# Another order for the 48 steps of a turn of the heads

## The chip, the cores and the metric

The kernel runs on one core of a Trainium2 chip. The metric is the device time of one execution in microseconds, taken as the median of several runs. A profiled execution shows where that time goes: TensorE (PE) does the matrix products, VectorE (DVE), ScalarE (ACT) and GpSimd (POOL) the rest, and SyncE (SP) issues nearly all DMAs. Each engine works through its own instructions in the order in which they are written, and they meet only at semaphores.

## The reference, cut to what matters

The layer is `x + attention(layernorm(x)) + experts(layernorm(x))` for x of 2 x 2048 x 512. The attention has 16 heads of width 128. Its queries, keys and values go through a causal convolution of four taps and a silu, and then a recurrence over the 2048 positions (a gated delta rule):

```
def step(S, inps):
    qt, kt, vt, at, bt = inps
    Sk = jnp.einsum('bhvk,bhk->bhv', S, kt)
    err = Sk - vt
    S = at[..., None, None] * S - bt[..., None, None] * (err[..., None] * kt[:, :, None, :])
    ot = jnp.einsum('bhvk,bhk->bhv', S, qt)
    return (S, ot)
```

The output `ot` is normalised over its 128 channels, multiplied by a sigmoid gate and projected by Wo. The experts are a mixture of 16, four for each of 512 tokens.

## The kernel before, in words

`prepare` normalises and turns x, computes the gates alpha and beta, and does the experts. `heads` does the attention, and `project` most of the product with Wo. The change is in the order of `heads` alone.

**Turns.** `heads` treats one head of one batch row at a time (32 heads in all), each in four groups (g = 0 to 3) of 512 positions. A turn is one such group, so there are 128, and a few turns around them that fill and drain the pipeline. In the loop three heads, twelve turns, are written out. The recurrence is computed in chunks of 128 positions, four in a group. Inside a chunk it becomes the inverse of a triangular 128 x 128 matrix and a few products, and from chunk to chunk the state S (128 x 128) is carried.

**Stages.** A turn works on several groups at once, each at another stage: `proj` is four groups ahead of the chain, `inv` three, `mid` two, `late` one, `chain` is the current group, and `ln` is one group behind. So what a turn computes is used in a later step of the same turn or in one of the next turns.

**Steps.** Each turn has 48 steps (`STEPS`), and every engine's `turn` function runs over all 48 and looks at each step which of its operations stand there. The constants in lines 54 to 79 say so: `L_AT = 22` puts the product L at TensorE's step 22. A step is a place in an engine's queue, and no time: two engines that are at the same step number are not at the same moment, unless a semaphore makes it so. Within one step the operations follow in the order of the code.

**TensorE** issues in each step one projection matmul of 512 columns (`project_some`, L1540): 48 for the four projections of a group, 12 each, three for each of four blocks of rows (high x high, high x low, low x high parts). Twelve projections fill a bank; its three banks are taken again when the convolution or the tanh has read them. Around these stand:
- the chain (`chain_step`, L1629 to L1659), 12 links, three for each of the four chunks c. Link 3c: the product of S and k (L1629), after which VectorE forms R (L1273). Link 3c+1: the product of R and TT (L1642), then q_gamma with S (L1647) into the output bank, after which ScalarE copies Wc (L1449). Link 3c+2: the product of Wc and k_rows (L1653) and of Wc and AT (L1659), after which VectorE updates S (L1286) and ScalarE copies the output `o` (L1456). `CHAIN` gives the step of each link.
- two visits of small products for the triangular inverse (`visit`): visit 0 (L1594, L1605, L1616) waits for the transpose `Tnb` (L1294), visit 1 (L1597, L1608, L1619) for what follows from visit 0 one turn earlier. Visit 0 is preceded by its waits and by that step's projection.
- A (`A_AT`, L1669), the turned keys (`KT_AT`, L1688) and values (`VT_AT`, L1694), L (`L_AT`, L1705), and the turned normalised output (`ON_TURN_AT`, L1716).

**The 16 x 16 block inverse** goes round through several engines. TensorE makes L, VectorE LT (L1351), ScalarE copies its diagonal blocks (`DIAG_AT`, L1400), GpSimd masks and adds them to Lc (`LC_AT`, L1170 and L1174), SP stores Lc into DRAM (`base_d`, L977, twice), waits for the stores, and loads it back spread over the partitions as Lb (L983). GpSimd solves with it in 15 pairs of small operations (`SOLVE_AT`, L1158 and L1165; a pair depends on the one before) and writes TTb (`T16P_AT`, L1180). VectorE transposes it to Tnb (`T16_AT`, L1294), which visit 0 needs. A late step of `SOLVE_AT` (over 24) works on the group loaded in that turn, an early one on the group of the turn before.

**GpSimd** also computes the power for the normalisation (`POW_AT`, `hrstd`, L1186), q_gamma (`QG_AT`, L1192), the gated output oG (`OG_AT`, L1200) and, in four places over two groups, the low parts of the next head's weights (`CUT_AT`, L1142; ScalarE's high parts, L1362, stand at the same steps). VectorE's normalised output `on` (`ON_AT`, L1318) waits for the power.

**ScalarE** further makes the first tap (`TAP_AT`, L1466 and L1468), kT, qT and vT, the sigmoid gate, diag_b (`DIAGB_AT`, L1393), the turned output oT (`OT_AT`, L1491), the value rows, and copies of the inverse's blocks (`PLACE_AT`, `TN_PLACE_AT`, `MT32_AT`, `TT64_AT`, `MT64_AT`, `TT128_AT`).

**SP** issues in each turn, in this order: gamma and scale when the chain has let them go, beta when diag_b is made, alpha when decay is made, the base blocks (two stores, a wait, one load), the next weights in one of four turns, and the store of oG.

GpSimd's operations stand in this form in its `turn`:

```
for s in range(STEPS):
    if s in SOLVE_AT and (proj if s > STEPS // 2 else inv):
...
    if proj and s == LC_AT:
...
    if inv and s == T16P_AT:
...
    if ln and s == POW_AT:
```

Of the kernel before, what the change touches and what calls it, by code (L numbers as in the profile page):

```python
# [50 lines left out]
LEAD = 0  # L51
PE_SLOT = 0

CHAIN = {2: 0, 5: 1, 10: 2, 12: 3, 16: 4, 22: 5, 24: 6, 27: 7, 31: 8, 37: 9, 42: 10, 47: 11}
PJ_OF = [[0, 1, 2, 0], [1, 2, 0, 1], [2, 0, 1, 2], [0, 1, 2, 1]]
PJ_FREED = [[(1, 0), (1, 3), (1, 2), (0, 0)], [(1, 1), (1, 2), (1, 3), (0, 0)],
            [(1, 1), (1, 2), (1, 3), (0, 0)], [(1, 1), (1, 2), (1, 3), (0, 1)]]
A_AT, KT_AT, VT_AT, ON_TURN_AT, L_AT = 12, 4, 14, 30, 22
VISIT_AT = {28: 0, 2: 1}
SOLVE_AT = {44: (0, 1), 45: (1, 4), 0: (4, 5), 3: (5, 6), 4: (6, 11), 5: (11, 13), 6: (13, 15)}  # L60
T16P_AT, POW_AT, QG_AT, OG_AT, DIAG_AT, LC_AT = 11, 13, 26, 40, 24, 22
AT_AT, K_AT, T16_AT, TN64_AT, DECAY_AT, LT_AT = 16, 7, 24, 9, 18, 22
BN_AT, AGGR_AT, ON_AT = 4, 11, 25
YB_AT, TT_AT = 38, 0
CONV_AT = {11: (0, 0), 12: (0, 1), 14: (0, 2), 26: (1, 0), 27: (1, 1), 30: (1, 2), 38: (2, 0), 42: (2, 1), 44: (2, 2)}
VSILU_AT, GATE_AT, DIAGB_AT, VROWS_AT, KSILU_AT, QSILU_AT, OT_AT = 3, 12, 7, 15, 18, 38, 31
PLACE_AT = {30: (0, 1), 14: (2, 3)}
TN_PLACE_AT = 1
MT32_AT, TT64_AT, MT64_AT, TT128_AT = 46, 5, 36, 3
O_AT = {7: 0, 22: 1, 38: 2, 2: 3}  # L70
TAP_AT = {7: 0, 25: 1, 38: 2}
TILES, TILE0 = 6, 4
TILE_CUT_AT = {25: (0, 1), 33: (1, 1), 42: (2, 1), 5: (3, 0)}
TILE_AT = 3
CUT_AT = {(3, 28): 0, (3, 34): 1, (3, 41): 2, (0, 22): 3}
ROUND_E, ROUND_T, RING = 4, 11, 3
EXPERT_AT = {0: 2, 3: 3, 6: 4, 8: 5}
WO_AT, W_AT = {1: 0, 3: 1, 5: 2, 7: 3}, 9
# [656 lines left out]
def heads(nc, bank, ident, pow_half, xT_hi_d, xT_lo_d, gates_d, base_d, oT_d, x_hi, x_lo, w_raw, w_cut, weights, taps, ln_w, ln_b,  # L735
# [10 lines left out]
    with ExitStack() as ctx:  # L746
# [466 lines left out]
        def _(dve):  # L1213
# [13 lines left out]
            def turn(dve, hh, g, n, chain, late, mid, inv, proj, ln, tile=None):  # L1227
                at = counter(hh, g)
                par, cur = (g + 1) % 2, g % 2
                for s in range(STEPS):  # L1230
# [27 lines left out]
                    if late and s == K_AT:  # L1258
# [4 lines left out]
                                          decay[:, (n + 1) % 3, 0:m, C:C + 1].to_broadcast([P, m, D]), ALU.mult).then_inc(k_done, 1)  # L1263
                    if chain and s in CHAIN:
                        k = CHAIN[s]
                        c, r = k // 3, k % 3
# [92 lines left out]
        def _(act):  # L1359
# [6 lines left out]
            def turn(act, hh, g, n, chain, late, mid, inv, proj, ln, tile=None):  # L1366
# [4 lines left out]
                for s in range(STEPS):  # L1371
# [66 lines left out]
                    if chain and s == TT128_AT:  # L1438

                        act.wait_ge(late_done, at(2, 1))  # L1440
                        for odd in range(2):
                            rows = slice(64, 128) if odd else slice(0, 64)
                            act.activation(TT[0:64, n % 3, odd::2, 64:128], w64[rows], ACT.Copy, scale=-1.0)\
                               .then_inc(tt128_done, 1)
                    if chain and s in CHAIN and CHAIN[s] % 3 == 1:
                        k = CHAIN[s]
                        act.wait_ge(chain_done, at(12, 0, k + 1))
# [62 lines left out]
        def _(pe):  # L1510
            def turn(pe, hh, g, n, chain, late, mid, inv, proj, ln, tile=None):
# [151 lines left out]
                for s in range(STEPS):  # L1663
# [14 lines left out]
                    if s in VISIT_AT:  # L1678
                        visit(VISIT_AT[s])
                    if chain and s in CHAIN:  # L1680
                        chain_step(CHAIN[s])
                    if late and s == KT_AT:
# [202 lines left out]
```

## Time and profile before

| | |
|---|---|
| median of 3 runs | 3532.4 us (3527.67 to 3541.74) |
| the profiled execution's own time | 3523.38 us |
| its span | 3521.8 us |
| mean granted TensorE clock | 0.995 |
| busy: PE, DVE, ACT, POOL | 98%, 68%, 67%, 55% of the span |
| `prepare`, before the first projection of the heads | 417.5 us |
| `heads`, its 128 turns and the drain | 417.5 to 3228 us |
| `project` | from 3228 us |

An instruction's record has its start and its length. The matmuls are pipelined, and a record of one covers more than its place in the queue: 512 columns are recorded with 0.39 to 0.48 us and follow one another every 0.23 us. So the distances between starts are read, and not the lengths. "Idle before" is time in which the engine had nothing running ahead of an instruction, and the name behind it is what ended the wait.

### The profile page before, as it was taken

To read this page: it belongs to the slowest core of one execution; us is meant where nothing else is said; L and a number is where in the kernel's file an instruction comes from. 1 tells how busy PE (TensorE), PEld (TensorE's weight loads), DVE (VectorE), ACT (ScalarE), POOL (GpSimd) and SP (SyncE) were. 2 spreads that over 40 slices of the span, in tenths; PEclk is the share of its full clock that TensorE was granted. 3 is DMA by queue.
4 is the path that set the end of the run, shared out by engine and by line. 5 is a ranking of instruction groups with operands and counts; after the bars stand their busy time and mean duration, and the time that the engine had idled before them with its cause. 6 is when DMAs were issued, how large, how long until landed. Compare 5 with 4: busy or idle time off the path is not lost. (4 is left out here: it accounts for less than half of the span.)

```text
span 3521.8 us, 105822 instructions
## 1 busy us (share of the span) xinstructions
PE 3444.3 (98%) x32308; PEld 2888.2 (82%) x32308; DVE 2401.3 (68%) x5785; ACT 2352.4 (67%) x6448; POOL 1927.6 (55%) x4905
## 2 busy tenths in 40 slices
PE   8999989999999999999999999999999999999998
PEld 7788768888888888888888888888888888877887
DVE  6656557777777777777777777777777777753222
ACT  4443467777777777777777777777777777762111
POOL 3323256666666666666666666666666666653000
PEclk9999999999999999999999999999999999999999
DMA  8654433333333333333533333333333333444543
GB/s 309 222 194 152 168 84 80 78 86 86 83 77 80 78 83 83 77 77 80 149 101 84 82 78 77 80 78 81 85 79 77 80 81 86 115 151 135 146 145 101
DMA packets 427683, 375.91 MB, mean 107 GB/s; under 512 B 191984, under 2 KB 323056, under 8 KB 421248
## 3 DMA queue, kind: packets, MB, share of 16 engines
q1 hardware_dynamic: 424000, 362.46, 37.8%
q8 instruction: 261, 4.28, 0.5%
q0 software_dynamic: 2080, 6.82, 0.5%
q14 instruction: 286, 2.34, 0.2%
q10 hardware_dynamic: 1056, 0.02, 0.0%
HBM read 292.62 MB, written 76.58 MB: 105 GB/s over the span
## 5 line engine op out<-in xcount | busy, mean ns | idle before, releaser
L1332 DVE SCALAR_TENSOR_TENSOR conv<-bank,tap,conv 128x512 f32<-128x512 f32 x1152 | 863.5, 750 | 183.8 <-ACT conv L1468 159.5
L1158 POOL TENSOR_TENSOR prods<-Lb,Tc 128x60 f32<-128x60 f32 (+14 forms) x1920 | 482.8, 251 | 557.3 <-DMA Lb<-base_d 413.5
L1540 PE MATMUL bank<-hx_hi,w_lo 128*128 128x512 f32 x1536 | 663.5, 432 | 0.0
L1540 PE MATMUL bank<-hx_lo,w_hi 128*128 128x512 f32 x1536 | 644.3, 419 | 14.4 <-DVE Tnb L1294 14.4
L1540 PE MATMUL bank<-hx_hi,w_hi 128*128 128x512 f32 x1536 | 645.5, 420 | 0.0
L1165 POOL TENSOR_TENSOR Tc<-Tc,prods 128x56 f32<-128x56 f32 (+13 forms) x1792 | 462.2, 258 | 141.1 <-POOL prods L1158 1.6
L1540 PEld LDWEIGHTS bank<-hx_lo,w_hi 128*128 128x128 f32 x1536 | 292.5, 190 | 45.6 <-DVE Tnb L1294 16.5
L1540 PEld LDWEIGHTS bank<-hx_hi,w_lo 128*128 128x128 f32 x1536 | 292.5, 190 | 31.9
L1540 PEld LDWEIGHTS bank<-hx_hi,w_hi 128*128 128x128 f32 x1536 | 293.0, 191 | 30.7 <-DVE conv L1332 6.1
L1400 ACT ACTIVATE same<-LT 32x128 f32<-32x128 f32 x512 | 157.4, 307 | 180.8 <-DVE LT L1351 171.5
L1468 ACT ACTIVATE conv<-bank,tap 128x512 f32<-128x512 f32 x384 | 264.0, 687 | 12.5
L1273 DVE SCALAR_TENSOR_TENSOR R<-bank,scale_c,v_rows 128x128 f32<-128x128 f32 x480 | 166.5, 347 | 145.3 <-PE bank L1629 145.2
L1286 DVE SCALAR_TENSOR_TENSOR S<-S,gamma,bank 128x128 f32<-128x128 f32 x480 | 162.5, 339 | 144.3 <-PE bank L1653 143.2
L1456 ACT ACTIVATE o<-bank 128x128 f32<-128x128 f32 x512 | 142.0, 277 | 142.8 <-PE bank L1659 134.6
L1142 POOL TENSOR_TENSOR w_lo<-w_raw,w_hi 128x512 fp32r<-128x512 f32 x152 | 195.2, 1285 | 75.9 <-ACT w_hi L1362 74.4
L1540 PE MATMUL bank<-x_hi,w_lo 128*128 128x512 f32 x512 | 223.7, 437 | 1.5 <-issue 0.3
L1540 PE MATMUL bank<-x_hi,w_hi 128*128 128x512 f32 x512 | 215.9, 422 | 2.9 <-issue 1.4
L1540 PE MATMUL bank<-x_lo,w_hi 128*128 128x512 f32 x512 | 215.2, 420 | 1.5 <-DVE Tnb L1294 1.5
L1653 PEld LDWEIGHTS bank<-Wc,k_rows 128*128 128x128 f32 x960 | 181.5, 189 | 37.5 <-ACT Wc L1449 1.9
L1642 PEld LDWEIGHTS bank<-R,TT 128*128 128x128 f32 x960 | 170.8, 188 | 50.4 <-DVE R L1273 23.7
L1629 PEld LDWEIGHTS bank<-S,kT 128*128 128x128 f32 x960 | 169.9, 189 | 39.7 <-DVE S L1286 9.9
L1200 POOL TENSOR_TENSOR oG<-oT,gT 128x512 f32<-128x512 f32 x128 | 165.3, 1291 | 62.7 <-ACT oT L1491 62.7
(211 smaller groups left out, 8880.3 us busy)
## 6 DMA issues: line engine op xcount, KB each, us to landing
Lb<-base_d SPq DMA_DIRECT2D x128, 512.0 KB, 4.7
gamma<-gamma_d SPq DMA_DIRECT2D x128, 258.0 KB, 3.6
alpha<-alpha_d SPq DMA_DIRECT2D x128, 256.0 KB, 3.2
oT_d<-oG SPq DMA_DIRECT2D x128, 256.0 KB, 4.2
gu_raw<-in_gate_up SPq DMA_DIRECT2D x16, 1408.0 KB, 6.4
o_raw<-oT_d SPq DMA_DIRECT2D x13, 1024.0 KB, 6.9
w_raw<-oT_d SPq DMA_DIRECT2D x12, 1024.0 KB, 7.2
dn_raw<-in_down SPq DMA_DIRECT2D x44, 256.0 KB, 6.9
```

Source lines behind the costliest of these rows:

```text
L1142: pool.tensor_tensor(w_lo[:, i], w_raw[:, i], w_hi[:, i].bitcast(F32), ALU.subtract).then_inc(wlo_done, 1)
L1158: pool.tensor_tensor(prods[:, :, i + 1:], Lb[:, i, :, i + 1:], Tc[:, :, i:i + 1].to_broadcast([P, G, SB - 1 - i]), ALU.mult)\
L1165: pool.tensor_tensor(Tc[:, :, i + 1:], (sel if i == 0 else Tc)[:, :, i + 1:], prods[:, :, i + 1:], ALU.subtract).then_inc(solve_done, 1)
L1200: pool.tensor_tensor(oG[:], oT[:], gT[:, (n - 1) % 6], ALU.mult).then_inc(oG_done, 1)
L1273: dve.scalar_tensor_tensor(out=R[:], in0=CO[:, 0:D], scalar=scale[:, cur, c:c + 1], in1=v_rows[:, cur, c], op0=ALU.mult, op1=ALU.add)\
L1286: dve.scalar_tensor_tensor(out=S[:], in0=S[:], scalar=gamma[:, cur, c, C:C + 1], in1=CO[:, 2 * D:3 * D], op0=ALU.mult, op1=ALU.add)\
L1332: dve.scalar_tensor_tensor(out=conv[i][:, to], in0=PJ[PJ_OF[g][i]][:], scalar=tap[:, i, j + 1:j + 2], in1=conv[i][:, to], op0=ALU.mult, op ...
L1468: act.activation(conv[i][:, KS - 1:], PJ[PJ_OF[g][i]][:], ACT.Copy, scale=tap[:, i, 0:1])\
L1540: last = pe.matmul(dst, a[:, i, k], b[:, k], start=(j == 0), stop=(j == 3 * KC - 1))
L1629: pe.matmul(CO[:, 0:D], kT[:, n % 6, chunk(c)], S[:], start=True, stop=True).then_inc(chain_done, 1)
L1642: pe.matmul(CO[:, D:2 * D], TT[:, n % 3, c], R[:], start=True, stop=True)\
L1653: pe.matmul(CO[:, 2 * D:3 * D], k_rows[:, cur, c], Wc[:], start=True, stop=True)\
```

## The change

Only constants change: the step of each operation in a turn, for all engines. The operations, their operands, their number and the semaphores that they wait for stay. The stages and the loops stay too.

```diff
-CHAIN = {2: 0, 5: 1, 10: 2, 12: 3, 16: 4, 22: 5, 24: 6, 27: 7, 31: 8, 37: 9, 42: 10, 47: 11}
+CHAIN = {3: 0, 7: 1, 11: 2, 14: 3, 16: 4, 18: 5, 21: 6, 25: 7, 34: 8, 37: 9, 41: 10, 47: 11}
...
-A_AT, KT_AT, VT_AT, ON_TURN_AT, L_AT = 12, 4, 14, 30, 22
-VISIT_AT = {28: 0, 2: 1}
-SOLVE_AT = {44: (0, 1), 45: (1, 4), 0: (4, 5), 3: (5, 6), 4: (6, 11), 5: (11, 13), 6: (13, 15)}
-T16P_AT, POW_AT, QG_AT, OG_AT, DIAG_AT, LC_AT = 11, 13, 26, 40, 24, 22
-AT_AT, K_AT, T16_AT, TN64_AT, DECAY_AT, LT_AT = 16, 7, 24, 9, 18, 22
-BN_AT, AGGR_AT, ON_AT = 4, 11, 25
-YB_AT, TT_AT = 38, 0
-CONV_AT = {11: (0, 0), 12: (0, 1), 14: (0, 2), 26: (1, 0), 27: (1, 1), 30: (1, 2), 38: (2, 0), 42: (2, 1), 44: (2, 2)}
-VSILU_AT, GATE_AT, DIAGB_AT, VROWS_AT, KSILU_AT, QSILU_AT, OT_AT = 3, 12, 7, 15, 18, 38, 31
-PLACE_AT = {30: (0, 1), 14: (2, 3)}
-TN_PLACE_AT = 1
-MT32_AT, TT64_AT, MT64_AT, TT128_AT = 46, 5, 36, 3
-O_AT = {7: 0, 22: 1, 38: 2, 2: 3}
-TAP_AT = {7: 0, 25: 1, 38: 2}
+A_AT, KT_AT, VT_AT, ON_TURN_AT, L_AT = 16, 1, 15, 34, 23
+VISIT_AT = {35: 0, 3: 1}
+SOLVE_AT = {38: (0, 1), 39: (1, 2), 40: (2, 7), 41: (7, 10), 42: (10, 12), 44: (12, 13), 5: (13, 14), 14: (14, 15)}
+T16P_AT, POW_AT, QG_AT, OG_AT, DIAG_AT, LC_AT = 15, 11, 23, 34, 23, 16
+AT_AT, K_AT, T16_AT, TN64_AT, DECAY_AT, LT_AT = 16, 0, 29, 7, 19, 27
+BN_AT, AGGR_AT, ON_AT = 0, 3, 28
+YB_AT, TT_AT = 43, 1
+CONV_AT = {12: (0, 0), 14: (0, 1), 16: (0, 2), 31: (1, 0), 32: (1, 1), 34: (1, 2), 37: (2, 0), 38: (2, 1), 43: (2, 2)}
+VSILU_AT, GATE_AT, DIAGB_AT, VROWS_AT, KSILU_AT, QSILU_AT, OT_AT = 1, 28, 14, 16, 17, 41, 28
+PLACE_AT = {26: (0, 1), 18: (2, 3)}
+TN_PLACE_AT = 0
+MT32_AT, TT64_AT, MT64_AT, TT128_AT = 39, 5, 47, 1
+O_AT = {15: 0, 22: 1, 36: 2, 0: 3}
+TAP_AT = {10: 0, 22: 1, 33: 2}
...
-CUT_AT = {(3, 28): 0, (3, 34): 1, (3, 41): 2, (0, 22): 3}
+CUT_AT = {(3, 19): 0, (3, 29): 1, (3, 34): 2, (0, 19): 3}
```

## Rows read from the trace of the kernel before

**Rows 1.** Busy time by stretch, steady part: us, PE, PEld, DVE, ACT, POOL, PEclk, DMA
```profile
600.00:3010.00 2410.00, 2388.99 (x25787) 2024.19 (x25786) 1832.94 (x4785) 1880.62 (x5468) 1555.78 (x4216) 1.00 0.34 84
```

**Rows 2.** Waits of PE, 600 to 3010 us: total us, times, longest us
```profile
PE bank L1716 <- DVE on L1318: 13.5, 13, 1.7
PE bank L1540 <- DVE Tnb L1294: 4.4, 7, 0.9
```

**Rows 3.** Line 1170, 600 to 3010 us: ns min/median/max, first and last start
```profile
L1170 POOL TENSOR_TENSOR same<-same,same_c x114: 452/455/612, 615.0 to 3004.5; 128x128 f32<-128x128 f32 x114
```

**Rows 4.** Timeline of PE, visit 0 of two turns twelve apart: start, us
```profile
2522.23 0.42 PE L1594 MATMUL bank<-Tnb,LT 32*32 32x32 f32 x28
...
2773.52 0.42 PE L1594 MATMUL bank<-Tnb,LT 32*32 32x32 f32 x28
```

**Rows 5.** Timelines of POOL, DVE, PE and SP in a good turn
```profile
1649.09 0.24 POOL L1158 TENSOR_TENSOR prods<-Lb,Tc 128x4 f32<-128x4 f32 x1
...
1649.87 0.46 POOL L1180 TENSOR_TENSOR TTb<-Tc,same_c 128x128 f32<-128x128 f32 x1 [0.23 <-POOL Tc L1165]
...
1651.35 1.11 DVE L1318 TENSOR_SCALAR on<-o,hmv,hrstd 128x128 f32<-128x128 f32 x4
...
1652.01 0.42 PE L1594 MATMUL bank<-Tnb,LT 32*32 32x32 f32 x28
...
1653.51 0.60 PE L1716 MATMUL bank<-ident,on 128*128 128x128 f32 x4
...
1653.20 1.29 SPq L977 DMA_DIRECT2D base_d<-Lc  x2
1655.79 0.56 SPq L983 DMA_DIRECT2D Lb<-base_d  x1
```

**Rows 6.** Timelines of SP, POOL, DVE and PE around a bad turn
```profile
1737.94 1.23 SPq L977 DMA_DIRECT2D base_d<-Lc  x2
1741.87 0.56 SPq L983 DMA_DIRECT2D Lb<-base_d  x1
...
1757.45 1.02 POOL L1186 TENSOR_TENSOR hrstd<-hveps,pow_half 128x4 f32<-128x4 f32 x1
...
1759.25 1.19 POOL L1192 TENSOR_TENSOR q_gamma<-qT,gamma 128x512 f32<-128x512 f32 x1
...
1758.51 3.24 DVE L1318 TENSOR_SCALAR on<-o,hmv,hrstd 128x128 f32<-128x128 f32 x4 [0.67 <-POOL hrstd L1186]
...
1761.99 1.09 PE L1716 MATMUL bank<-ident,on 128*128 128x128 f32 x4 [1.75 <-DVE on L1318]
```

**Rows 7.** Busy time by stretch, just after that wait; the clock is third from last
```profile
1762.00:1766.00 4.00, 4.00 (x15) 3.58 (x16) 2.26 (x4) 2.32 (x6) 1.51 (x2) 0.60 0.52 135
```

**Rows 8.** Timelines of PE, DVE and ACT in the good turn, links of the chain
```profile
1650.95 0.40 PE L1540 MATMUL bank<-hx_hi,w_hi 128*128 128x512 f32 x1
1651.19 0.40 PE L1642 MATMUL bank<-R,TT 128*128 128x128 f32 x2
...
1650.71 0.34 DVE L1273 SCALAR_TENSOR_TENSOR R<-bank,scale_c,v_rows 128x128 f32<-128x128 f32 x1
...
1646.64 0.38 PE L1642 MATMUL bank<-R,TT 128*128 128x128 f32 x2
...
1647.06 0.28 ACT L1449 ACTIVATE Wc<-bank 128x128 f32<-128x128 f32 x1
```

**Rows 9.** Timelines of ACT in the good and the bad turn
```profile
1654.15 0.78 ACT L1491 ACTIVATE oT<-bank,lnb,lnw 128x512 f32<-128x512 f32 x1 [0.40 <-PE bank L1716]
...
1758.12 0.69 ACT L1468 ACTIVATE conv<-bank,tap 128x512 f32<-128x512 f32 x1
...
1758.86 0.63 ACT L1362 ACTIVATE w_hi<-w_raw 128x512 fp32r<-128x512 f32 x1
```

**Rows 10.** Waits of PE, 417 to 600 us
```profile
PE bank L1540 <- DVE Tnb L1294: 11.4, 3, 7.4
```

**Rows 11.** Waits of PE, 3010 to 3230 us
```profile
PE bank L1716 <- DVE on L1318: 4.0, 4, 1.4
```

## The prediction

> **What bounds the kernel now.** I read the busy time by stretch first, then TensorE's waits in each stretch, then the period of a turn, then an undisturbed turn and a late one side by side. In the steady part of the heads TensorE is busy 2389.0 of 2410.0 us with its clock at 1.00 [rows 1]: it is the bound, and its work is the same in both orders. An order can only win what TensorE does not work, or works at the lower clock. The waits name it: 13.5 us in 13 waits for `on` (the normalised output, L1318) before the four transposes of L1716, and 4.4 us in 7 waits for `Tnb` (L1294) before the small solving matmuls [rows 2]. L1170 runs once a turn: 113 turns from 615.0 to 3004.5 us are 21.15 us each [rows 3]. Twelve turns without such a wait, from 2522.23 to 2773.52 us, are 20.94 us each [rows 4]. So 0.21 us a turn, 113 x 0.21 = 24 us in all, is lost in a few bad turns; 20.94 us is the floor.
>
> What a bad turn is: in a good one [rows 5] GpSimd ends the block inverse with pair 14 (from 1649.09) and the write of TTb (1649.87 to 1650.33), then runs the power (`hrstd`, L1186; 1.02 us) to 1651.3, and VectorE starts `on` at 1651.35. `on` ends at 1652.46 and TensorE takes it at 1653.51: room 1.05 us. The matmuls of visit 0 start at 1652.01, 1.68 us after TTb is written. In a bad turn [rows 6] the load of the base blocks was issued 3.93 us after their stores (1737.94 to 1741.87), where the good one needs 2.59 (1653.20 to 1655.79): 1.34 us late. The thirty solving operations follow the load one by one, and in the next turn the power, which starts at 1757.45, is late by as much. Then comes a second loss: `on` takes 3.24 us for 1.12, since `q_gamma` starts on GpSimd at 1759.25 and runs beside it. TensorE waits 1.75 us, and its granted clock falls to 0.60 in the next four microseconds (1.2 GHz for a part of them) [rows 7].
>
> That row bears on a rule of the Trainium skill, SBUF — State Buffer, section "SBUF: two separate sides": VectorE in a two-port mode and GpSimd take one port pair in turn, each for a whole instruction. The trace agrees, by those 3.24 us.
>
> **The change, part by part.** Nothing is added or removed; only places of steps in each engine's queue move, and with them the waits.
>
> 1. *The solve.* GpSimd's pairs stood at 44, 45, 0, 3 to 6 and all before the power (13). Now pairs 0 to 12 stand at 38 to 44, pair 13 at 5, the power at 11, pair 14 at 14, TTb at 15, then Lc, q_gamma (23), oG (34). The load starts the pairs, as before. The product before it (L on TensorE) is at 23 instead of 22, a mean step of 20.94/48 = 0.44 us later, so masking, store, load and solve move by the same 0.44. But the power no longer stands behind pair 14 and TTb (1649.09 to 1650.33, 1.24 us). In the times of the good turn it ends at 1651.31 + 0.44 - 1.24 = 1650.5, and TTb is ready at 1650.33 + 0.44 + 1.02 = 1651.8.
> 2. *The users.* `on` is at 28 and `Tnb` behind it at 29 (before: Tnb 24, on 25), both after LT (27), which now ends at 1650.71 + 0.44 = 1651.15 (R followed it at 1650.71 [rows 8]). So VectorE has `on` from 1651.2 to 1652.3. The transposes move from 30 to 34: four projections more (0.23 each, the slot from 1650.95 to 1651.19), one step of the chain more (about 0.5) and visit 0 less (1653.51 - 1652.01 less two projections, 1.04), so 1653.51 + 0.92 + 0.5 - 1.04 = 1653.9. Visit 0 (35) follows at 1654.6. The room for a late power grows from 1.1 us to 1653.9 - 1650.5 - 1.1 = 2.3; that for a late TTb, less 0.3 for the transpose, from 1.4 to 1654.6 - 1651.8 - 0.3 = 2.5. A load late by 1.34 us fits into both.
> 3. *The collision.* q_gamma followed the late power by 0.8 us (1758.47 to 1759.25 [rows 6]). Now pair 14 and TTb stand between too, 1.24 us more, and `on` is over. Left are collisions with operations of 0.2 and 0.46 us, at most 0.9.
>
> Worth: 24 us of bad turns, less 2 left in some ten late ones (0 to 5): **-22 us**.
>
> 4. *Weight cuts.* GpSimd's cuts in the last group move from 28, 34, 41 to 19, 29, 34, the fourth from 22 to 19. The last no longer stands between the load and its solve; the ScalarE parts move alike. But ScalarE now has, between the transposes (34) and the copy `o` of chunk 2 (36): 0.64 from the transposes' start (1653.51 to 1654.15), oT 0.78, a cut 0.63, the tap 0.90 with its 0.20 us copy, a cut 0.63, the copy 0.28 and its release 0.1 [rows 9], 4.0 us end to end and 3.5 as they overlap; TensorE overwrites that bank at 41, 3.6 us after the transposes (seven projections, visit 0, three chain pairs). 0 to 0.4 us in 32 of 128 turns: 0 to 13 us. I take **+2**, near 3.5, since overlap is what the row shows (a tap of 0.69 and a Wc of 0.28 take 0.74, 1758.12 to 1758.86).
> 5. *The chain.* Its closest pairs were three steps apart and are now 16 to 18, with only two projections between. Needed: 0.42 (1646.64 to 1647.06) for the matmul, 0.28 for Wc, and 0.14 of release (R ends at 1651.05, L1642 starts at 1651.19), 0.84 us; there are 0.90 to 0.95 (0.82 from L1642 to visit 0 with one projection, and 0.23 more, less the 0.1 to 0.15 of entering the visit) [rows 8]. It fits if ScalarE is free: by then it has the tap, diag_b and a copy behind it since projection 11, 2.5 us of work in 4. I take 0 (0 to 0.1 in 128 turns, 0 to 13 us). The k_rows product (7 to 0) and the transposes before it (4 to 1) stand ahead of the chain's first R on VectorE; BN, k_rows, TTb, Tnb and R are 2.6 us and done about 0.3 us before TensorE asks at 7: 0.
> 6. *DMA queue.* SP's issues keep their order (gamma, scale, beta, alpha, base, oG). Beta waits for diag_b (7 to 14), alpha for decay (18 to 19), the oG store for oG (40 to 34). Each is used a turn or more later; hidden by that turn. If late, the base store behind alpha is the first to suffer.
> 7. *Start and end.* While the pipeline fills, Tnb costs 11.4 us in three waits [rows 10]. Visit 0 seven steps later puts 7 x 0.23 = 1.6 us of projections into the first; the others come a whole loop after it, with the same work between. **-1.6** (0 to -5). In the tail four waits for `on` cost 4.0 us [rows 11]; **-1** (-4 to +1).
>
> Sum: -22 + 2 - 1.6 - 1 = -22.6, about -22 us, against the profiled execution's own 3523.4. The median of the runs shown is 9 us above that; from 3532.4 the same sum gives **3510 us**.
>
> **The rivals.**
> - *Late stays late.* The load depends on Lc, Lc on GpSimd's last solve. From the load's issue to the end of the power it is 16.6 us (1741.87 to 1758.47 [rows 6]), from store to load 2.59 [rows 5], and the masking and Lc take 0.8: 20.0 us of a 20.9 us turn, in both orders. If lateness sums up over turns, less than half of the 22 is won: 3532 - 10 = 3522. For it: only 0.9 us a turn is recovered. Against: a bad turn is followed by good ones in the trace.
> - *The rule of the ports, for this order.* `on` now runs beside pair 14 and TTb in every turn. With 0.9 us of collision it ends at 1653.2, still ahead of 1653.9. In a turn with a load 1.34 us late it ends at 1650.5 + 1.34 + 1.1 + 0.9 = 1653.85, at the edge; some 0.4 us of wait in each of ten such turns: 3514. (The rule is the one cited above; it speaks against putting `on` there.)
> - *Small waits.* Parts 4 and 5 at half their bounds, +13 for my +2: 3521.
> - *Slower.* Place: ScalarE at the chain's step 16, behind diag_b (moved from 7 to 14) and the copy of chunk 0 (7 to 15). If it comes there later than TensorE, Wc waits and nothing lies between 16 and 18 to cover it: every microsecond is TensorE's. It decides from about 1.5 us of ScalarE lateness; with 0.35 us more, 128 x 0.35 = 45 us, less 22: 3555. For it: ScalarE works 1880.6 of 2410.0 us [rows 1] and the cuts fill it further in the last group. Against: at step 16 it is not.
>
> **How the numbers follow.** Forecast 0.45, late stays late 0.17, ports 0.10, small waits 0.15, slower 0.13. Low end: all 24, 5 and 4 us won from 3532, and 9 more if unprofiled runs have more bad turns: 3490. High end: nothing won and both small waits: 3536; only the slower rival and a little more lie outside. 0.5% is 17.7 us, about what a measurement of this kernel can tell: faster below 3514.7. Forecast nearly all, half of the ports and a little of the rest: 0.52. Slower 0.12, the rest 0.36.
>
> **What would show it.** Right: the waits of TensorE for `on` and `Tnb` in the steady part fall from 17.9 to under 4 us, no `on` over 2.5 us beside q_gamma, no clock loss there, 12 turns still 251.3 us. Wrong: TensorE idle before L1653 (ScalarE's Wc) or before L1659/L1647 (the copy `o`) by more than 5 us in all, a floor above 21.0, or the same 13 waits under another name.

## The result, and the profile after

The changed kernel takes **3482.2 us** (median of 6 runs, 3477.24 to 3483.19), the kernel before 3537.1 us beside it (6 runs, 3527.67 to 3548.68). The ratio is 0.9842, with a 95% interval of 0.9825 to 0.9858. The change was right in its sign, and the time lies under the low end of the predicted range, 3490 us. The profiled execution of the changed kernel took 3482.47 us with a span of 3480.9 us, its median; that of the kernel before 3523.38 us, 13.7 us under its new median. So the profiles account for 41 of the 55 us. The other 14 are in no trace: the runs before spread over 21 us and the changed ones over 6, which would fit a number of bad turns that varies from one execution to the next, but that is argued and not shown.

TensorE's busy time in the steady part of the changed kernel, in the columns of [rows 1]:

```profile
600.00:3010.00 2410.00, 2408.86 (x26220) 2065.55 (x26219) 1821.38 (x4865) 1907.86 (x5556) 1577.90 (x4291) 1.00 0.36 85
```

It is idle for 1.1 us where [rows 1] leave 21.0. The list of its waits in this stretch is empty: against [rows 2], neither `on` nor `Tnb` is there. L1170, once a turn (ns min/median/max, first and last start), against [rows 3]:

```profile
L1170 POOL TENSOR_TENSOR same<-same,same_c x116: 447/461/466, 613.3 to 3007.0; 128x128 f32<-128x128 f32 x116
```

115 turns in 2393.7 us are 20.81 us each, for 21.15. Visit 0 of two turns twelve apart, against [rows 4]:

```profile
1115.14 0.42 PE L1594 MATMUL bank<-Tnb,LT 32*32 32x32 f32 x28
...
1364.69 0.42 PE L1594 MATMUL bank<-Tnb,LT 32*32 32x32 f32 x28
```

That is 249.55 us, 20.80 a turn, where undisturbed turns took 20.94. This is what the prediction had ruled out.

A good turn of the changed kernel (timelines of GpSimd, VectorE, TensorE and SP), against [rows 5]:

```profile
901.76 1.01 POOL L1186 TENSOR_TENSOR hrstd<-hveps,pow_half 128x4 f32<-128x4 f32 x1
...
903.46 0.56 POOL L1180 TENSOR_TENSOR TTb<-Tc,same_c 128x128 f32<-128x128 f32 x1 [0.22 <-POOL Tc L1165]
...
903.35 1.26 DVE L1318 TENSOR_SCALAR on<-o,hmv,hrstd 128x128 f32<-128x128 f32 x4
...
905.87 0.60 PE L1716 MATMUL bank<-ident,on 128*128 128x128 f32 x4
...
905.74 1.27 SPq L977 DMA_DIRECT2D base_d<-Lc  x2
...
908.32 0.58 SPq L983 DMA_DIRECT2D Lb<-base_d  x1
```

The power ends 3.1 us ahead of the transposes (902.77 to 905.87); less 1.26 for `on`, which also had LT to wait for, 1.84 us are free, and before it was 1.05. The same rows two turns later, where the load is issued 4.30 us after its stores (2.58 is normal), against [rows 6]:

```profile
947.12 1.26 SPq L977 DMA_DIRECT2D base_d<-Lc  x2
...
951.42 0.57 SPq L983 DMA_DIRECT2D Lb<-base_d  x1
...
965.84 1.02 POOL L1186 TENSOR_TENSOR hrstd<-hveps,pow_half 128x4 f32<-128x4 f32 x1
...
967.55 0.50 POOL L1180 TENSOR_TENSOR TTb<-Tc,same_c 128x128 f32<-128x128 f32 x1 [0.23 <-POOL Tc L1165]
...
968.83 1.18 POOL L1192 TENSOR_TENSOR q_gamma<-qT,gamma 128x512 f32<-128x512 f32 x1
...
966.89 1.26 DVE L1318 TENSOR_SCALAR on<-o,hmv,hrstd 128x128 f32<-128x128 f32 x4 [1.24 <-POOL hrstd L1186]
...
968.39 0.63 PE L1716 MATMUL bank<-ident,on 128*128 128x128 f32 x4
```

The load is 1.72 us late, more than in [rows 6], and the power starts late enough for VectorE to wait 1.24 us. But `on` ends at 968.15, before q_gamma starts, and takes 1.26 us, not 3.24. TensorE comes for it at 968.39, and the whole turn takes 21.29 us, less than half a microsecond over its usual 20.82. The granted clock stays at 1.00.

Late loads have not become rarer. Of the turns 8 to 123 twelve follow a load that was issued over 3.2 us after its stores (2.59 is the median), and none of these twelve is longer than 21.3 us. In the kernel before there are seven such turns, and they take 22.7 to 25.0 us.

While the heads fill, TensorE waits 11.1 us in three waits for Tnb, for the 11.4 of [rows 10]. In the tail the four waits for `on` [rows 11], 4.0 us, are one of 0.5.

### The profile page after: what moved, and what is told of

The parts are those of the page before. It is cut to its first block and busy times, and to the rows that moved or that the text cites. A ratio compares the mean times of both kernels' runs of the same rounds, so it can differ in the third digit from the quotient of the medians.

```text
span 3480.9 us, 105791 instructions
## 1 busy us (share of the span) xinstructions
PE 3426.1 (98%) x32308; PEld 2900.5 (83%) x32308; DVE 2353.1 (68%) x5785; ACT 2348.0 (67%) x6448; POOL 1921.0 (55%) x4905
## 5 line engine op out<-in xcount | busy, mean ns | idle before, releaser
L1332 DVE SCALAR_TENSOR_TENSOR conv<-bank,tap,conv 128x512 f32<-128x512 f32 x1152 | 854.6, 742 | 57.0 <-ACT conv L1468 47.0
L1540 PE MATMUL bank<-hx_hi,w_lo 128*128 128x512 f32 x1536 | 652.1, 425 | 11.1 <-DVE Tnb L1294 11.1
L1540 PE MATMUL bank<-hx_hi,w_hi 128*128 128x512 f32 x1536 | 655.7, 427 | 0.8 <-DVE conv L1332 0.8
L1540 PE MATMUL bank<-hx_lo,w_hi 128*128 128x512 f32 x1536 | 637.1, 415 | 0.0
L1540 PEld LDWEIGHTS bank<-hx_hi,w_lo 128*128 128x128 f32 x1536 | 292.3, 190 | 43.2 <-DVE Tnb L1294 12.4
L1540 PEld LDWEIGHTS bank<-hx_hi,w_hi 128*128 128x128 f32 x1536 | 293.1, 191 | 29.3 <-DVE conv L1332 0.9
L1540 PEld LDWEIGHTS bank<-hx_lo,w_hi 128*128 128x128 f32 x1536 | 292.4, 190 | 29.9
L1449 ACT ACTIVATE Wc<-bank 128x128 f32<-128x128 f32 x512 | 142.0, 277 | 208.1 <-PE bank L1642 199.9
L1540 PE MATMUL bank<-x_hi,w_hi 128*128 128x512 f32 x512 | 218.4, 427 | 2.0 <-PEq L151 1.0
L1540 PE MATMUL bank<-x_hi,w_lo 128*128 128x512 f32 x512 | 217.6, 425 | 0.0
L1540 PE MATMUL bank<-x_lo,w_hi 128*128 128x512 f32 x512 | 213.0, 416 | 0.0
L1642 PEld LDWEIGHTS bank<-R,TT 128*128 128x128 f32 x960 | 180.7, 189 | 36.5 <-DVE R L1273 0.4
L1659 PE MATMUL bank<-Wc,AT 128*128 128x128 f32 x1024 | 197.8, 275 | 0.0
```

The lines of the kernel that those rows point to most:

```text
L1332: dve.scalar_tensor_tensor(out=conv[i][:, to], in0=PJ[PJ_OF[g][i]][:], scalar=tap[:, i, j + 1:j + 2], in1=conv[i][:, to], op0=ALU.mult, op ...
L1540: last = pe.matmul(dst, a[:, i, k], b[:, k], start=(j == 0), stop=(j == 3 * KC - 1))
L1642: pe.matmul(CO[:, D:2 * D], TT[:, n % 3, c], R[:], start=True, stop=True)\
L1659: pe.matmul(OB[:], AT[:, cur, c], Wc[:], start=first, stop=True).then_inc(out_done, 1)
```

## The experiments

The table has, beside each median, the ratio to the kernel before on the same chip, and three readings of the trace that the runs need. A turn is 48 projections, so every 48th start of L1540 opens one; the four figures are the median length of a turn in us by its place among the four of a head (first, second, third, last), over turns 8 to 123, and the sum is those 116 turns.

| kernel | us | ratio | first, second, third, last | sum |
|---|---|---|---|---|
| before | 3537.1 | 1 | 21.00, 20.99, 20.87, 21.20 | 2453.4 |
| changed | 3482.2 | 0.9842 | 20.63, 20.92, 20.82, 20.70 | 2414.5 |
| changed, other chip | 3478.3 | 0.9859 | 20.60, 20.91, 20.78, 20.69 | 2412.1 |
| before + `on` used later | 3538.4 | 1.0049 | 21.39, 21.04, 20.92, 21.32 | 2467.1 |
| before + power ahead of pair 14 | 3539.8 | 1.0057 | 21.18, 21.02, 21.23, 20.80 | 2464.0 |
| before + q_gamma later | 3613.8 | 1.0278 | 22.39, 21.01, 20.87, 22.88 | 2535.8 |
| before + visit 0 and Tnb later | 3641.5 | 1.0342 | 22.18, 22.09, 21.98, 21.90 | 2556.1 |
| before + visit 0 later | 3600.2 | 1.0198 | 21.20, 21.35, 21.23, 21.12 | 2528.2 |
| before + new cuts | 3565.7 | 1.0124 | 21.23, 21.00, 20.86, 22.51 | 2490.3 |
| before + delayed load | 3568.1 | 1.0127 | 21.00, 21.01, 22.67, 20.79 | 2491.5 |
| changed + delayed load | 3494.4 | 0.9912 | 20.60, 20.92, 20.92, 20.70 | 2426.0 |
| changed, power back | 3541.2 | 1.0053 | 20.92, 20.91, 20.78, 21.13 | 2460.5 |
| changed, cuts back | 3493.7 | 0.9911 | 21.12, 20.92, 20.82, 20.70 | 2429.9 |
| changed, third cut back | 3486.5 | 0.9901 | 20.93, 20.91, 20.78, 20.69 | 2421.1 |
| changed, fourth cut back | 3477.7 | 0.9876 | 20.61, 20.91, 20.78, 20.69 | 2413.4 |
| changed, chain back | 4172.7 | 1.1826 | 23.87, 27.22, 26.91, 27.41 | 3056.3 |
| changed, link 3 later | 3480.0 | 0.9859 | 20.65, 20.91, 20.79, 20.68 | 2413.8 |

The kernel before took 3522 to 3526 us (medians) on the chips of the experiments. The half width of a ratio's interval is 0.0016 to 0.0029, but 0.0050 with q_gamma later.

### One part of the change, put into the old order

**`on` used later.**

```diff
-ON_TURN_AT 30, OT_AT 31
+ON_TURN_AT 34, OT_AT 35
```

> The kernel before, with only TensorE's transposes of the normalised output moved from step 30 to 34 and ScalarE's copy of them from 31 to 35. If the room behind the power is what counts, the 13.5 us of waits for `on` in the steady part mostly go (the 4.4 us for Tnb stay), and the time falls by 15 to 22 us (ratio 0.994 to 0.996). If lateness only moves to the next turn, or q_gamma's collision is what costs, it falls by under 8 us.

TensorE's waits, 600 to 3010 us:

```profile
PE bank L1659 <- ACT Wc L1449: 2.8, 17, 0.2
...
PE bank L1716 <- DVE on L1318: 1.0, 3, 0.5
```

The waits for `on` are gone, and the kernel is 0.5% slower. The expected gain of 15 us or more is missed. The turns with cuts are longer (first 21.39, last 21.32). Of the 0.39 us that the first turn is longer, 0.32 are lost by its step 2, by the starts of L1540, so they come over from the last turn of the head before, where the transposes and the turned output behind them now stand beside ScalarE's weight cuts and a Wc. That ScalarE is the cause is argued from these places; no run here separates it.

**The power ahead of pair 14.**

```diff
-SOLVE_AT ... 6: (13, 15);  T16P_AT 11
+SOLVE_AT ... 6: (13, 14), 14: (14, 15);  T16P_AT 15
```

> The kernel before, with only GpSimd's order changed: the power stands before pair 14 and TTb (steps 13, 14, 15), as in the new order; nothing moves on the other engines. Room theory: waits for `on` fall, but TTb is 1.0 us later with visit 0 still at step 28, so waits for Tnb grow in every late turn; sum between -10 and +15 us. If it were the power's place alone that brought the gain, the ratio would be near 0.99.

```profile
PE bank L1540 <- DVE Tnb L1294: 16.0, 25, 2.1
...
PE bank L1716 <- DVE on L1318: 0.4, 1, 0.4
```

In the listed waits it is a trade: 13.5 us for `on` [rows 2] became 16.0 us for Tnb. In time the kernel is 17.6 us above the one before, a little over the expected 15. Whichever of the two GpSimd does second is late, as long as visit 0 stays at 28.

**q_gamma later.** This is no part of the change, which moves q_gamma the other way (26 to 23). It takes the collision away by itself.

```diff
-QG_AT 26
+QG_AT 41
```

> The kernel before, with only q_gamma moved behind oG on GpSimd (26 to 41), so that it can't run beside a late `on`. Collision theory: no `on` over 2 us remains, waits for `on` fall from 13.5 to about 5 us and the clock loss goes, ratio 0.993 to 0.996. Room theory alone: under 5 us either way. It can also lose, where q_gamma now delays the solve in turns with weight cuts.

```profile
PE bank L1659 <- ACT Wc L1449: 45.0, 27, 1.7
```

```profile
1719.74 0.72 ACT L1484 ACTIVATE qT<-conv,tap 128x512 f32<-128x512 f32 x1 [2.12 <-POOL q_gamma L1192]
```

With q_gamma away no `on` is over 587 ns and no wait for `on` is listed. But ScalarE writes the next qT at step 38 and may do so only when q_gamma has read the old one; in the turns with cuts it stood 2.12 us for it (the second row, a timeline of ScalarE), with Wc behind it in its queue, and TensorE behind Wc. The kernel loses 2.8%. That the waits for `on` go with the collision is shown; what the collision costs in time is not, since the new wait hides it.

**Visit 0 later, first try.**

```diff
-VISIT_AT {28: 0, ...};  T16_AT 24;  YB_AT 38;  MT64_AT 36
+VISIT_AT {35: 0, ...};  T16_AT 29;  YB_AT 43;  MT64_AT 47
```

> The kernel before, with only visit 0 moved from step 28 to 35 and what hangs on it (Tnb 24 to 29, behind `on`; Yb 38 to 43; MT64 36 to 47). Room theory: the waits for Tnb (4.4 us and the short ones of 0.15 us in g = 0) go, while those for `on` stay or fall a little because TensorE comes 1 us earlier to the transposes: they grow. Time between -10 and +30 us. If the floor of 20.94 us a turn falls to 20.8 here, visit 0's place is what set it; if it stays, it is the chain's spacing.

TensorE's waits, and VectorE in one turn:

```profile
PE bank L1540 <- DVE Tnb L1294: 56.7, 106, 0.7
```

```profile
1717.09 1.11 DVE L1318 TENSOR_SCALAR on<-o,hmv,hrstd 128x128 f32<-128x128 f32 x4 [0.28 <-POOL hrstd L1186]
...
1718.88 1.54 DVE L1332 SCALAR_TENSOR_TENSOR conv<-bank,tap,conv 128x512 f32<-128x512 f32 x2 [0.67 <-ACT conv L1468]
1720.33 0.30 DVE L1294 STREAM_TRANSPOSE Tnb<-TTb 128x128 f32<-128x128 f32 x1
```

Tnb moved behind two convolution steps on VectorE (26 and 27), which stand at 31 and 32 in the changed kernel. The edit tested that and not visit 0, and this theory was neither confirmed nor refuted by it.

**Visit 0 later, with Tnb at its place.**

```diff
-VISIT_AT {28: 0, ...};  YB_AT 38;  MT64_AT 36
+VISIT_AT {35: 0, ...};  YB_AT 43;  MT64_AT 47
```

> The old order with visit 0 alone moved from step 28 to 35 (with the copies that follow it, yB to 43 and MT64 to 47); Tnb stays at 24 on VectorE, ahead of on, which the earlier try of this had moved behind two convolutions. Theory: the bad turns are of the wait for on, which VectorE does after Tnb, so they stay: waits for on of 10 us or more, those for Tnb under 1 us, and 3517 to 3525 us. Rival: visit 0's old place was the reason, since it stands ahead of the transposes in the queue and costs room there: the transposes now come 1 us earlier in time and the waits for on grow to 20 us or more, 3530 us or more. Third: the floor of a turn falls to 20.80 us by visit 0's place: 3505 to 3512 us.

```profile
PE bank L1716 <- DVE on L1318: 48.6, 37, 4.3
```

The rival held. Visit 0 had given `on` some of its room: without it ahead, TensorE is at the transposes 1 us earlier, and a late power costs that much more. A second loss was expected by none: the second and third turns are 0.36 us longer without any listed wait. By the starts of L1540, 0.38 of it is lost between steps 30 and 32, where the transposes (30) and link 8 (31) stand. Links 7 (27) and 8 had visit 0 between them as cover; in the changed kernel they stand at 25 and 34. That the missing cover is the reason is argued from these places.

**The weight cuts at their new places.**

```diff
-CUT_AT = {(3, 28): 0, (3, 34): 1, (3, 41): 2, (0, 22): 3}
+CUT_AT = {(3, 19): 0, (3, 29): 1, (3, 34): 2, (0, 19): 3}
```

> The old order with only the weight cuts at their new places (19, 29, 34 in the last group, 19 in the first). In the run with the cuts back at their old places only the first turn of each head was longer, 21.12 for 20.60 us. Theory: ScalarE's cut at step 41 makes it late until the chain's link 1 in the next turn, in both orders. Then the first turn's median falls here from 21.00 to 20.5 to 20.7 us, the others stay at 20.99, 20.87 and 20.8 to 21.2, and the time is 9 to 14 us under the kernel before. Rival 1: the cuts' new places pay only in the new order, since here ScalarE at 29 and 34 has oT (31) and the diagonal copies too: the first turn's median falls by less than 0.1 us or the last one's rises by 0.3, and the time is 0 to 15 us above. Rival 2: GpSimd's third cut, no longer between the load and its solve, also takes bad turns away: 20 us or more under.

TensorE's waits; then GpSimd, VectorE and TensorE in a last turn of a head; then the stretch behind (PE, PEld, DVE, ACT, POOL, clock, DMA):

```profile
PE bank L1716 <- DVE on L1318: 34.6, 29, 1.7
```

```profile
1775.94 1.02 POOL L1186 TENSOR_TENSOR hrstd<-hveps,pow_half 128x4 f32<-128x4 f32 x1
1776.93 1.27 POOL L1142 TENSOR_TENSOR w_lo<-w_raw,w_hi 128x512 fp32r<-128x512 f32 x1
...
1776.99 3.24 DVE L1318 TENSOR_SCALAR on<-o,hmv,hrstd 128x128 f32<-128x128 f32 x4 [0.67 <-POOL hrstd L1186]
...
1780.48 1.09 PE L1716 MATMUL bank<-ident,on 128*128 128x128 f32 x4 [1.75 <-DVE on L1318]
```

```profile
1780.00:1784.00 4.00, 3.52 (x13) 3.22 (x14) 2.75 (x5) 0.78 (x1) 1.39 (x2) 0.57 0.36 97
```

The theory and Rival 2 have the sign wrong, and Rival 1 has the sign but not the size, 42 us for 0 to 15. GpSimd's cut at 19 starts right behind the power in all 29 last turns, and in 27 of them `on` starts with it: the collision of [rows 6], now without any late load. `on` takes the same 3.24 us: of its four pieces, 0.34 us each when undisturbed, one takes 1.29 beside the cut and one 1.21 beside q_gamma. TensorE waits the same 1.75 us, and its granted clock is 0.57 in the four microseconds behind. The last turn is 1.3 us longer. In the changed kernel pair 14 and TTb stand between the power and that cut.

### The late load, made on purpose

A small store of Lc into a DRAM buffer of its own, and a wait for its landing, between the stores and the load of the base blocks, in one of four turns. It moves the load by 1.5 us, 32 times. (Lines are shifted by 5: L1323 is L1318.)

```diff
+if g == 1:
+    sp.dma_start(extra_d, Lc).then_inc(extra_stored, 16)
+    sp.wait_ge(extra_stored, ...)
```

> The kernel before, with the load of the base blocks made late by one more small store and its landing (about 1.9 us) in one group of four (g = 1, 32 times), which adds no work to any other engine. Room theory: each of these costs what a bad turn costs, 1.5 to 4 us (q_gamma's collision and the clock included): 50 to 120 us over the kernel before.

> The changed kernel with the same late load in one group of four. Room theory: 2.3 us of room takes 1.9 us; under 0.7 us each, 0 to 20 us over the changed kernel, so a ratio to the kernel before still near 0.985 to 0.99. Rival (the floor alone brought the gain, and late loads cost the same in both orders): 50 us and more over the changed kernel.

Waits of TensorE, the old order and then the new:

```profile
PE bank L1721 <- DVE on L1323: 24.1, 30, 1.5
PE bank L1545 <- DVE Tnb L1299: 18.1, 30, 1.3
```

```profile
PE bank L1721 <- DVE on L1323: 3.9, 5, 1.7
```

The turn behind the delay (the third) grows from 20.87 to 22.67 us in the old order and from 20.78 to 20.92 in the new. Over the 116 turns that is 38 us against 12 to 14: with 29 delays in them 1.3 us each against 0.4 to 0.5. The first expectation is missed by a little (45 us over the kernel before, for 50 to 120); the second held (16 us over the changed kernel), and its rival is refuted.

### One part of the change, taken back

**The power behind pair 14 and TTb again.**

```diff
-SOLVE_AT ... 14: (14, 15);  T16P_AT 15, POW_AT 11
+SOLVE_AT ... 9: (14, 15);  T16P_AT 10, POW_AT 11
```

> The changed kernel with GpSimd's power put back behind pair 14 and TTb (steps 9, 10, 11), all else as changed. The power then ends 1.24 us later, at about the moment when `on` starts. Room theory: 1.1 us of room is still there behind it, so good turns cost nothing, and the few turns with loads late by 1.3 us or more lose 0.3 to 2 us each: 0 to 15 us over the changed kernel. If the power's place was the key, 25 us and more.

Waits of TensorE; the durations of `on` (ns min/median/max); GpSimd, VectorE and TensorE in one bad turn:

```profile
PE bank L1716 <- DVE on L1318: 18.6, 10, 3.0
```

```profile
L1318 DVE TENSOR_SCALAR on<-o,hmv,hrstd x452: 334/343/1304, 614.4 to 2991.0; 128x128 f32<-128x128 f32 x151
```

```profile
1664.54 1.02 POOL L1186 TENSOR_TENSOR hrstd<-hveps,pow_half 128x4 f32<-128x4 f32 x1
...
1666.35 1.26 POOL L1142 TENSOR_TENSOR w_lo<-w_raw,w_hi 128x512 fp32r<-128x512 f32 x1
1667.57 1.17 POOL L1192 TENSOR_TENSOR q_gamma<-qT,gamma 128x512 f32<-128x512 f32 x1
...
1665.60 3.23 DVE L1318 TENSOR_SCALAR on<-o,hmv,hrstd 128x128 f32<-128x128 f32 x4 [2.12 <-POOL hrstd L1186]
...
1669.07 0.63 PE L1716 MATMUL bank<-ident,on 128*128 128x128 f32 x4 [2.99 <-DVE on L1318]
```

This one edit gives all of the gain back, and the time is 0.5% above the kernel before. The power is late by pair 14 and TTb, and what follows it on GpSimd is no longer pair 14 and TTb but the mask, a cut and q_gamma, beside which `on` takes 3.23 us. But the ten listed waits are not all of it. The median first and last turns of a head are 0.32 and 0.44 us longer than in the changed kernel, which in 29 heads is 22 of the 48 us. There `on` and Tnb end about 0.8 to 1 us later, and by the starts of L1540 TensorE loses the time at steps 34 to 36, in stretches too short for the list.

**The cuts.** All four back; the third alone; the fourth alone:

```diff
-CUT_AT = {(3, 19): 0, (3, 29): 1, (3, 34): 2, (0, 19): 3}
+CUT_AT = {(3, 28): 0, (3, 34): 1, (3, 41): 2, (0, 22): 3}
...
+CUT_AT = {(3, 19): 0, (3, 29): 1, (3, 41): 2, (0, 19): 3}
...
+CUT_AT = {(3, 19): 0, (3, 29): 1, (3, 34): 2, (0, 22): 3}
```

> The changed kernel with the weight cuts at their old steps (28, 34, 41 in the last group, 22 in the first) on ScalarE and GpSimd. If the cuts' places brought the part of the gain in g = 3 and g = 0 (24 us of bad turns had six of about 0.9 us there), this loses 5 to 12 us; if the room behind the power takes it anyway, under 3 us.

> The changed order with the third cut alone at its old step, 41 instead of 34 in the last group. Theory: this one is the cause of the long first turn. Its median goes from 20.60 to 21.0 to 21.15 us, the others stay, and the time is 12 to 16 us above the changed kernel's 3478. Rival: the first cut (28) or the fourth (22) is the cause; then this one is 0 to 3 us above.

> The changed order with the fourth cut alone at its old step, 22 instead of 19 in the first turn of a head. Theory (the third is the cause): 0 to 3 us above the changed kernel, first turn 20.60 to 20.7 us. Rival: it stands beside the copy of chunk 1 (22) and the diagonal copies on ScalarE and ahead of q_gamma on GpSimd, and costs 0.1 us or more in each of 32 turns at steps 22 to 34: 3 to 10 us above.

The first expectation asked 5 to 12 us for all four cuts; they cost 15.4 in the medians. The second asked 12 to 16 us for the third alone, its rival 0 to 3; it is 8.2. The fourth changes nothing (-0.7), as its theory had it.

In the traces the cuts' places are worth 17.8 us in the new order (sums 2429.9 and 2412.1), nearly all of it in the first turn of a head, 21.12 for 20.60 us. No listed wait shows it; the list leaves out waits as short as these. ScalarE and the starts of TensorE do, from the last turn of a head into the first. With the cuts back, the next turn starting at 1747.76:

```profile
1746.96 0.71 ACT L1484 ACTIVATE qT<-conv,tap 128x512 f32<-128x512 f32 x1
1747.57 0.62 ACT L1362 ACTIVATE w_hi<-w_raw 128x512 fp32r<-128x512 f32 x1
1748.22 0.57 ACT L1437 ACTIVATE MT<-bank 64x128 f32<-64x128 f32 x2
...
1752.42 0.28 ACT L1449 ACTIVATE Wc<-bank 128x128 f32<-128x128 f32 x1
...
1751.15 0.40 PE L1540 MATMUL bank<-x_lo,w_hi 128*128 128x512 f32 x1
1751.54 0.46 PE L1638 MATMUL bank<-v_rows,TT 128*128 128x128 f32 x2
```

The changed kernel on the other chip, the turn starting at 1741.62:

```profile
1740.83 0.71 ACT L1484 ACTIVATE qT<-conv,tap 128x512 f32<-128x512 f32 x1
1741.57 0.57 ACT L1437 ACTIVATE MT<-bank 64x128 f32<-64x128 f32 x2
...
1745.93 0.28 ACT L1449 ACTIVATE Wc<-bank 128x128 f32<-128x128 f32 x1
...
1744.90 0.40 PE L1540 MATMUL bank<-x_lo,w_hi 128*128 128x512 f32 x1
1745.13 0.38 PE L1638 MATMUL bank<-v_rows,TT 128*128 128x128 f32 x2
```

ScalarE has no idle time from the first to the last of its lines, so the cut of 0.62 us at step 41 goes through to link 1's Wc: 4.66 us into the turn, for 4.31 (in the median over all first turns 4.65 for 4.16). Link 1 (L1638 in the first chunk of a head) also needs ScalarE's copies of TT. It starts 0.39 us behind the projection before it, for 0.23, and the record of that projection, 0.40 us long, covers the wait. Over all first turns TensorE is behind the changed kernel by 0.12 us at step 4, 0.35 at step 8 and 0.51 at step 15, and by no more after that.

The third cut alone costs 9.0 us of the 17.8 (2421.1 less 2412.1), but not in this way. With it alone at 41, link 1's Wc is at 4.17 us, where the changed kernel has it, and TensorE loses nothing up to step 14. What is late there is GpSimd: its own third cut, at 41 again, stands among the pairs of the solve and takes 1.3 us there, the power ends 13.35 us into the first turn for 12.18, Tnb at 15.18 for 14.10, and 0.24 of the 0.33 us are lost ahead of the projection of step 35, where TensorE waits for visit 0's inputs. So ScalarE's lateness at link 1 needs the first two cuts at their old places as well, and the 17.8 us are no sum of single cuts. The first two were not tried alone.

**The chain.** The links and the copies `o` back at their old steps; then, as a try at an improvement, link 3 one step later:

```diff
-CHAIN = {3: 0, 7: 1, 11: 2, 14: 3, ...};  O_AT = {15: 0, 22: 1, 36: 2, 0: 3};  VT_AT 15
+CHAIN = {2: 0, 5: 1, 10: 2, 12: 3, ...};  O_AT = {7: 0, 22: 1, 38: 2, 2: 3}
...
+CHAIN = {3: 0, 7: 1, 11: 2, 15: 3, ...};  VT_AT 14
```

> The changed order with the twelve links of the chain and the four copies of the output back at their old steps; the solve, the power, visit 0 and the cuts stay at the new ones. Theory: the undisturbed turns are faster (20.80 for 20.94 us) because the links stand elsewhere, and the bad turns are gone because of the power's and the users' places. Then the undisturbed turn comes back to 20.88 to 20.94 us, no bad turns come back, and the time is 10 to 17 us above the changed kernel's. Rival 1: the floor is of visit 0's place, seven steps later: 0 to 3 us above. Rival 2: the chain's places do matter for the late turns too, since VectorE's R stands between on and Tnb: waits for on or Tnb over 5 us in the steady part, and 20 us or more above.

> The changed order with link 3 of the chain at step 15 instead of 14, and the turned values at 14 instead of 15. In the first turn of each head link 3 waits for the state that VectorE has just updated, about 0.07 us in each of 30 turns by the profile. Theory: that wait goes and nothing takes its place: 2 to 3 us below the changed kernel, which five rounds can barely show. Rival: links 3 and 4 now stand one projection apart, less than R needs (0.42 for the matmul and 0.34 for R on VectorE), so link 4 waits 0.3 us or more in every turn: 40 us or more above.

TensorE's waits with the chain back, and VectorE and TensorE in one turn:

```profile
PE bank L1642 <- DVE R L1273: 191.6, 69, 2.8
PE bank L1653 <- ACT Wc L1449: 116.7, 91, 1.6
```

```profile
1706.64 0.87 DVE L1254 BATCH_NORM_STATS2 hstats<-o 128x6 f32<-128x128 f32 x4 [3.19 <-ACT o L1456]
...
1708.59 0.35 DVE L1273 SCALAR_TENSOR_TENSOR R<-bank,scale_c,v_rows 128x128 f32<-128x128 f32 x1
...
1709.09 0.47 PE L1642 MATMUL bank<-R,TT 128*128 128x128 f32 x2 [2.72 <-DVE R L1273]
```

The theory and both rivals missed this: the time is 694 us above the changed kernel. The statistics of `o` are at VectorE's step 0 in the changed order, and wait there 3.19 us for a copy that ScalarE has at step 2 again, behind copies that wait for visit 1; R of link 1 stands in the queue behind them. Every turn is 3 to 7 us longer. The run says that the chain's places and those of the other engines are one piece, and nothing on the floor. Link 3 later changes nothing (3480.0 for 3478.3), so its rival, 40 us for a wait at link 4, is refuted, and no version here beats the changed kernel.

**The changed kernel again.**

> The changed kernel itself, on the chip of the other experiments, so that they can be read against it. If the 1.6% is of the two orders, 3480 to 3487 us here, and the cuts back in their old places (3493.7) and the added delay (3494.4) did cost some 10 us each. Rival: part of the 1.6% was of the chip or of the hour, and the changed kernel stands here at 3490 to 3495; then those two edits cost nothing.

The theory held: 3478.34 us, ratio 0.9859 (0.9836 to 0.9882). Against it the cuts back (3493.7) and the added delay (3494.4) did cost, 15 and 16 us.

## Why the prediction was right or wrong

**The account.** Undisturbed, twelve turns in a row take 251.2 us before, 249.5 after, and 250.8 with the cuts back (the fastest twelve of each trace). Times 116/12 they give what the 116 turns would take with no bad one: 2428.3, 2411.8 and 2424.4 us. The rest of the sums is bad turns: 25.1, 2.7 and 5.5 us. So in the profiles the change took 22.4 us out of bad turns and 16.5 us out of all others. The prediction drew the line between the two in this way, but the traces have no sharp one: in the kernel before nine of the 29 last turns are 0.4 us longer than the shortest, with 0.2 us of it in the list at most. Drawn at the four medians of the table instead, 28.7 us come out of ordinary turns and 10.2 out of the rest.

1. *The solve, the users, the collision (-22).* The mechanism is right, and the size too, by the prediction's own line. The waits for `on` and Tnb went from 17.9 us to none listed, no `on` takes over 601 ns (1315 before), and the clock does not fall there. Against the turn's start the power ends 0.62 us earlier than before in the median (0.8 worked out), the transposes come 0.2 later (0.4 worked out), and `on` takes 1.26 for 1.11: room 1.84 us for the 2.3 I named. The delays made on purpose, the late loads that the changed kernel met by itself, and the power put back show that it is this place that decides. Two readings behind it were too narrow. The late load explains seven of the 13 bad turns, 18 of the 24 us; the other six, first and last turns of 21.8 to 22.0 us, have their load on time and the power 0.4 to 0.6 us late, for a reason that is not traced. And the 3.24 us of `on` in [rows 6] are not q_gamma's alone: one of its pieces takes 1.22 us beside q_gamma and the next 1.30 beside a weight cut.
2. *The weight cuts (+2).* Wrong in sign. I looked only at what the new places would cost, the copy `o` of chunk 2, and priced nothing of what the old ones cost: ScalarE without idle time from step 41 into the next turn, and the cut ahead of GpSimd's solve, which I named. They are worth -13 us by the fastest twelve, -18 by the sums, in the new order. It is the term with the largest miss. In the old order the same cuts cost 37 us in the 116 turns, so no price of theirs can be told without naming the order.
3. *The chain (0).* It can't be checked. Without the cuts 3.9 us of the floor are left (251.2 against 250.8), and they belong to all the other moves together. With only the power back the fastest twelve also take 250.8 us, so the parts of the floor do not add up one by one, and the run with the chain back could not tell the chain's own.
4. *The floor.* This is the step that failed. The prediction let an order win only what TensorE does not work or works at the lower clock, and took 20.94 us a turn for the floor because TensorE read 98% busy and twelve turns had no listed wait. The work is the same in both orders, but the measured floor is 20.80 us. The records of overlapping matmuls cover short waits between starts (above, 0.40 us recorded over a distance of 0.39 where 0.23 is enough), so TensorE read as busy while it lost 0.14 us a turn. Twelve turns without a listed wait are not twelve turns without waits.
5. *Start and end.* -1.6 predicted, -1.7 measured up to turn 8. As far as the waits show, that is luck: those for Tnb, which it was to shorten, went only from 11.4 to 11.1 us, and the same stretch varies by 3 us among the versions of the changed order. The drain and the projection behind it came out within 0.2 us of before, for -1, though the waits for `on` there fell by 3.5 us.
6. *The basis.* I subtracted 22 us from a median that was 9 us above the profile. The changed kernel's median is its profile (3482.2 and 3482.5), so the 9 us went too. If they were bad turns of other executions, an order that removes bad turns should remove them; no second trace of the kernel before shows whether they were. The prediction had them only as a reserve in the low end. Of the 28 us between 3510 and 3482, 19 are in the profiles, nearly all of them the floor and the cuts, and 9 are this.

**The rivals.** *Late stays late*: refuted; behind the late turn above the next one has its power 11.51 us after its start, for 11.19 in the median. *The ports in this order*: `on` beside pair 14 and TTb takes 1.26 us for 1.11, 0.15 for the 0.9 that this rival allowed, and it fits into the room. *Slower*: no wait for Wc appears. But its mechanism, ScalarE or VectorE late for a link and nothing to cover it, is what cost 2.8% with q_gamma later and 644 us in the 116 turns with the chain back. *Small waits*: the ordinary turns did not grow by 13 us, they shrank by 16.5.

## What to carry to other kernels

Read the floor from the distances between starts of the bound engine, by place in the loop, and compare places: before the change the first turn of a head stood 0.4 us and the last 0.5 us above what the changed order needs, mostly without a listed wait. Ask of an operation that moves what its old place cost, not only what the new one will. And expect little of single moves in such an order: the five edits that put one part of the change into the old order were all slower, by 0.5 to 3.4%, though all parts together win 1.6%.

## What the runs showed of the hardware

- One piece of `on` on VectorE (128x128) goes from 342 ns to about 1210 to 1320 ns beside GpSimd's q_gamma or a weight cut (both two inputs of 128x512), while GpSimd's operation keeps its 1.18 or 1.28 us. It is so for all 170 pieces of over 1 us in five traces (before, new cuts, power back, delayed load before, visit 0 alone later): the piece starts 21 to 261 ns after GpSimd's operation and ends 80 to 89 ns after its end. The Trainium skill, SBUF — State Buffer, section "SBUF: two separate sides", has a shared port pair that GpSimd or VectorE, in a two-port mode, holds for a whole instruction, whichever starts first. The traces agree with that, though none says in which mode `on` runs. In all these cases GpSimd started first, so they do not show what it would lose the other way round. In the changed kernel TTb starts within a piece of `on` in 96 of 116 turns; TTb takes 0.51 us in the median for 0.46, and `on` as a whole 1.26 for 1.11.
- The granted clock was 0.57 in the four microseconds behind a wait of 1.75 us (the old order with the new cuts), with 2.4 GHz as full and 1.2 GHz as the lower level. In the first try with visit 0 later TensorE waited 56.7 us in 106 waits of at most 0.7 us, and the granted clock was 1.00 from 600 to 3010 us.
